# Four alternating GRU chains and four gather buffers in the first stage of a graph network

## The reference

```
h = relu(layernorm(x));  x = x + segment_sum(h[src] * edge_weight, dst)       # round 1
feat = relu(layernorm(x))
4 times:  a = segment_sum((feat @ W[k].T + b[k])[etypes, src], dst)           # round 2
          r = sigmoid(i_r + h_r);  z = sigmoid(i_z + h_z)
          n = tanh(i_n + r * h_n);  feat = (1 - z) * n + z * feat
          # i_* = a @ w_ih.T + b_ih,  h_* = feat @ w_hh.T + b_hh
x = x + feat
```

## Time and profile before

| What | Value |
|---|---|
| Median of three runs | 6666.92 us |
| The profiled execution: its own time | 6632.5 us |
| Its span, first to last instruction | 6630.3 us |
| Busy over the span | PE 64%, DVE 66%, ACT 41%, POOL 64% |
| TensorE's mean granted clock | 0.854 |
| `norm` | 120 to 436 us |
| Node loop without summing, `j` up to 24 | 436 to 1181 us |
| Wait for the first gather of `h[src]` | 1181 to 1416 us |
| Node loop with summing, `j` from 25 | 1416 to about 2600 us |
| First gather of the next stage | 2614.5 us |

### The profile page before, as it was taken

One profiled execution on the slowest core, in us unless ns is written; L12 is line 12 of the kernel. 1 busy time (PEld: TensorE's weight loads), 2 busy tenths in 40 slices (PEclk: granted clock), 3 DMA queues, 4 the chain that ended last, 5 costly groups with the idle time before them and its releaser, 6 DMA issues. The chain is left out here.

```text
span 6630.3 us, 70235 instructions
## 1 busy us (share of the span) xinstructions
PE 4211.2 (64%) x13088; PEld 2105.9 (32%) x13088; DVE 4371.3 (66%) x6372; ACT 2717.9 (41%) x4465; POOL 4255.8 (64%) x3977
## 2 busy tenths in 40 slices
PE   0038888137777776888788788879978882012321
PEld 0014444013434433444344344434434441000110
DVE  3778888137878786777677677767865664455432
ACT  1346666025555554444454444445443331111000
POOL 2666677763333332777677677767767776774777
PEclk9999999568888887999999899999989995555555
DMA  2876554124444443333333333334445552222331
GB/s 82 290 243 209 199 193 162 29 69 142 146 148 140 155 134 121 115 115 118 96 117 114 100 112 116 114 108 140 139 124 133 147 149 79 72 74 77 109 99 57
DMA packets 701757, 843.04 MB, mean 127 GB/s; under 512 B 183377, under 2 KB 339524, under 8 KB 701646
## 3 DMA queue, kind: packets, MB, share of 16 engines
q1 hardware_dynamic: 572286, 716.54, 33.1%
q0 software_dynamic: 129360, 125.36, 8.5%
HBM read 420.11 MB, written 425.30 MB: 128 GB/s over the span
## 5 line engine op out<-in xcount | busy, mean ns | idle before, releaser
L380 POOL DMA_INDIRECT step_g<-f_rows,lab_i x1568 | 1732.3, 1105 | 657.2 <-issue 476.5
L753 POOL DMA_INDIRECT nd_g<-h_and_label,src_i x392 | 419.7, 1071 | 701.8 <-DVE sgn_t L1049 595.1
L1338 DVE COPY_PREDICATED step_msg<-step_mask,step_p_w 128x512 f32<-128x512 uint8 x588 | 427.6, 727 | 518.1 <-ACT step_p_w L1283 487.0
L1240 PE MATMUL step_p_w<-step_gT,wT 128*128 128x512 f32 x1568 | 748.9, 601 | 2.7 <-ACT step_gT L1252 2.7
L731 POOL DMA_INDIRECT nd_xg<-in_x,dst_i x392 | 446.4, 1139 | 389.9 <-DMA x_of_dst<-nd_xg 168.7
L771 PE MATMUL nd_p_r<-nd_fT,wT 128*128 128x512 f32 x588 | 356.3, 690 | 282.4 <-DVE nd_fT L1020 263.9
L1892 POOL DMA_INDIRECT out<-attend_o,last_i x392 | 404.9, 1033 | 178.0 <-issue 119.1
L380 POOL DMA_INDIRECT logits_g<-h_rows,lab_i x392 | 410.5, 1047 | 152.0 <-issue 119.1
L380 POOL DMA_INDIRECT typed_g<-h_rows,lab_i x392 | 403.9, 1030 | 156.7 <-issue 119.2
L744 POOL DMA_INDIRECT h_and_label<-slot,lab_at x392 | 406.8, 1038 | 123.3 <-issue 123.3
L906 ACT ACTIVATE nd_cand<-nd_pre,bias 128x512 f32<-128x512 f32 x392 | 281.9, 719 | 423.9 <-DVE nd_pre L1005 423.9
(11 more groups left out here) (272 smaller groups left out, 9852.6 us busy)
## 6 DMA issues: line engine op xcount, KB each, us to landing
f_rows<-nd_ro SPq DMA_DIRECT2D x294, 256.0 KB
h_rows<-nd_cen SPq DMA_DIRECT2D x98, 512.0 KB
step_mask<-masks SPq DMA_DIRECT2D x392, 128.0 KB
step_fT<-f_turned SPq DMA_DIRECT2D x196, 256.0 KB
f_turned<-step_fn SPq DMA_DIRECT2D x147, 256.0 KB, 2.1
f_rows<-step_rows SPq DMA_DIRECT2D x147, 256.0 KB
h_and_label<-nd_hx SPq DMA_DIRECT2D x49, 528.0 KB, 4.1
f_rows<-nd_h SPq DMA_DIRECT2D x49, 512.0 KB, 3.0
```

The lines of the kernel that those rows point to most:

```text
L380: nc.gpsimd.indirect_dma_start(out=g[:, c % RING, j, :], out_offset=None, in_=table, in_offset=bass.IndirectOffsetOnAxis(ap=idx[:, 8 * c + ...
L753: nc.gpsimd.indirect_dma_start(out=g[:, c % 2, j, :], out_offset=None, in_=m.ht, in_offset=bass.IndirectOffsetOnAxis(ap=m.src_i[:, 8 * c + ...
L1240: pe.matmul(p_w[k % 2][:], lhsT=m.wT[:, WK + k, :], rhs=gT[:, h], start=True, stop=True).then_inc(s_w, 1)
L1338: nc.vector.copy_predicated(msg[:, h], mask[:, h, k], p_w[k % 2][:]).then_inc(s_sel, 1)
```

## The change

The four steps of a pair are spread over two iterations. In iteration `j` the pair `one = j - 1` does its first two steps (stage FIRST) and the pair `two = j - 2` its last two (stage SECOND). The new `slot(k)` gives the stage, the step and the group of slot `k`: even slots are FIRST, odd ones SECOND, and the output of a slot is needed four slots later, or five where it passes to the second stage. So four chains alternate. Work tiles double, and semaphores exist once for each stage. `p_n` has one bank for each stage instead of each group; `p_r`, `p_z`, `p_out` stay single. The loop gets one more iteration at its end. Three orders change too: on DVE `update` is that of the slot before, behind this slot's `argument` and extras; on ACT the candidate stands behind the copy of rows; the addition to `x` and the third norm move from `j - 2` to `j - 3`, the first half of the addition into slot 7 (`add_x`). On POOL `xg` gets four buffers (`RING`), so that the gathers of a chunk wait for the store of the chunk four back instead of two back, and a count `s_moved` tells SP which chunk is in memory. The labels now start once the last store has landed.

```diff
+def slot(k):
+    return k % 2, k // 4, k // 2 % 2
...
-        xg = sb("xg", [P, 2, 8 * D])
+        xg = sb("xg", [P, RING, 8 * D])
...
             def store_x(c):
-                pool.wait_ge(s_xg[c % 2], landed(c, c % 2, 8))
-                nc.gpsimd.dma_start(m.xs[c], xg[:, c % 2]).then_inc(s_xgs[c % 2], 16)
+                pool.wait_ge(s_xg[c % RING], arrived(c, c % RING, 8))
+                nc.gpsimd.dma_start(m.xs[c], xg[:, c % RING]).then_inc(s_xgs[c % RING], 16)
+
+            def stored_x(c):
+                pool.wait_ge(s_xgs[c % RING], arrived(c, c % RING, 1))
+                pool.sem_inc(s_moved, 1)
...
             for c in range(C):
-                if c >= 2:
-                    pool.wait_ge(s_xgs[c % 2], 16 * (c // 2))
+                if c >= RING:
+                    stored_x(c - RING)
...
             store_x(C - 1)
+            for c in range(C - RING, C):
+                stored_x(c)
```

In PE's `body`:

```diff
             def body(j, summing):
-                gru, n2 = j - 1, j - 2
+                one, two = j - 1, j - 2
                 for q in range(8):
-                    if live(gru, NI):
-                        gates(gru, q)
-                    if q < 2 and live(n2, NI):
-                        turn_out(n2, q)
-                    if q >= 2 and live(gru, NI):
-                        turn_out(gru, q)
+                    stage, t, u = slot(q)
+                    if live(two if stage else one, NI):
+                        gates(two if stage else one, stage, t, u)
+                    stage, t, u = slot((q + 6) % 8)
+                    i = (two if stage else one) - (1 if q < 2 else 0)
+                    if live(i, NI):
+                        turn_out(i, stage, t, u)
```

In ACT's `body`:

```diff
                 for q in range(8):
-                    if live(gru, NI):
-                        gate(gru, q)
-                        if q >= 2:
-                            take_rows(gru, q)
+                    here = (two if q % 2 else one, *slot(q))
+                    if live(here[0], NI):
+                        gate(*here)
+                    stage, t, u = slot((q + 6) % 8)
+                    i = (two if stage else one) - (1 if q < 2 else 0)
+                    if live(i, NI) and not (stage == SECOND and t == 1):
+                        take_rows(i, stage, t, u)
+                    if live(here[0], NI):
+                        candidate(*here)
```

In DVE's `body`:

```diff
                 for q in range(8):
-                    if live(gru, NI):
-                        argument(gru, q)
+                    stage, t, u = slot(q)
+                    if live(two if stage else one, NI):
+                        argument(two if stage else one, stage, t, u)
+                    if q == 7 and live(two, NI):
+                        add_x(two, 0)
                     if live(n2, NI):
+                        if q == 1:
+                            add_x(n2, 1)
                         norm2(n2, q)
...
-                    if live(gru, NI):
-                        update(gru, q)
+                    stage, t, u = slot((q + 7) % 8)
+                    i = (two if stage else one) - (1 if q < 1 else 0)
+                    if live(i, NI):
+                        update(i, stage, t, u)
```

More of the change, by code:

```diff
@@ L431, in loop_nodes @@
 def loop_nodes(eng, body):
-    for j in range(3):
+    for j in range(4):
         body(j, False)
-    with eng.Fori(0, TURN - 5) as k:
-        body(k + 3, False)
+    with eng.Fori(0, TURN - 6) as k:
+        body(k + 4, False)
     body(TURN - 2, False)
@@ L486, in nodes_and_sum @@
         p_r, p_z = ps("p_r"), ps("p_z")
-        p_n = [ps(f"p_n{u}") for u in range(2)]
+        p_n = [ps(f"p_n{stage}") for stage in range(2)]
         p_in, p_out = ps("p_in"), ps("p_out")
@@ new lines, in handed_back @@
+                def handed_back(s):
+                    if stage == FIRST:
+                        if is_below(i, 1):
+                            if n > 0:
+                                pe.wait_ge(s[FIRST], n)
+                        elif not (is_below(i, 2) and before == 0):
+                            pe.wait_ge(s[SECOND], 4 * (i - 1) + before)
+                        else:
+                            pe.wait_ge(s[FIRST], n)
+                    elif live(i + 1, NI):
+                        pe.wait_ge(s[FIRST], 4 * (i + 1) + before + 1)
+                    elif n > 0:
+                        pe.wait_ge(s[SECOND], n)
@@ new lines, in gates @@
+                handed_back(s_r)
+                pe.matmul(p_r[:], lhsT=m.wT[:, HR, :], rhs=f, start=True, stop=True).then_inc(s_gr[stage], 1)
+                if not (is_below(i, 1) and before == 0):
+                    pe.wait_ge(s_pre[stage], n)
+                pe.matmul(p_n[stage][:], lhsT=m.wT[:, HN, :], rhs=f, start=True, stop=True).then_inc(s_gn[stage], 1)
+                handed_back(s_z)
+                pe.matmul(p_z[:], lhsT=m.wT[:, HZ, :], rhs=f, start=True, stop=True).then_inc(s_gz[stage], 1)
@@ new lines, in gate, with candidate @@
+                nc.scalar.activation(zg[:, stage, u], p_z[:], ACT.Sigmoid, bias=m.bias[:, B_Z:B_Z + 1]).then_inc(s_z[stage], 1)
+            def candidate(i, stage, t, u):
+                n = 4 * i + 2 * t + u
+                act.wait_ge(s_pre[stage], n + 1)
+                if not (is_below(i, 1) and t == 0):
+                    act.wait_ge(s_f[stage], n - 1)
+                nc.scalar.activation(cand[:, stage, u], pre[:, stage, u], ACT.Tanh, bias=m.bias[:, B_IN:B_IN + 1]).then_inc(s_cand[stage], 1)
@@ L914, in take_f0, with take_rows @@
+            def take_rows(i, stage, t, u):
+                act.wait_ge(s_to[stage], 4 * i + 2 * t + u + 1)
+                if stage == FIRST:
+                    if not (is_below(i, 1) and t == 0):
+                        act.wait_ge(s_ros[stage][u], 32 * i + 16 * t)
+                elif not is_below(i, 1):
+                    act.wait_ge(s_ros[stage][u], 16 * i)
+                nc.scalar.copy(ro[:, stage, u], p_out[:]).then_inc(s_ro[stage], 1)
             def take_f0(j, u):
@@ new lines, in update @@
+            def update(i, stage, t, u):
+                n = 4 * i + 2 * t + u
+                ch = Chain(dve, s_chg[stage], 2 * n)
+                if t == 0:
+                    f = fT[:, FIRST, u, 1, :] if stage == SECOND else f0T[:, u, :]
+                else:
+                    f = fT[:, stage, u, 0, :]
+                c, d = cand[:, stage, u], dif[:, stage, u]
+                dve.wait_ge(s_cand[stage], n + 1)
+                ch.then(nc.vector.tensor_tensor(d, f, c, ALU.subtract))
+                dve.wait_ge(s_z[stage], n + 1)
+                ch.then(nc.vector.tensor_tensor(d, d, zg[:, stage, u], ALU.mult))
+                if not is_below(i, 1):
+                    dve.wait_ge(s_to[stage], n - 3)
+                    if stage == FIRST and t == 1:
+                        dve.wait_ge(s_chg[SECOND], 2 * (4 * (i - 1) + u + 1))
+                nc.vector.tensor_tensor(fT[:, stage, u, t, :], d, c, ALU.add).then_inc(s_f[stage], 1)
@@ L1029, in norm2, with add_x @@
+            def add_x(i, u):
+                if u == 0:
+                    dve.wait_ge(s_xb, 32 + 16 * i if is_last(i, NI) else 16 * i + 16)
+                dve.wait_ge(s_to[SECOND], 4 * i + 3 + u)
+                half = xb[:, 8 * u:8 * u + 8].rearrange("p j d -> p (j d)")
+                nc.vector.tensor_tensor(half, half, p_out[:], ALU.add).then_inc(s_x2, 1)
+            def norm2(i, q):
                 if q == 2:
```

224 lines of the change are left out of this document (103 added, 121 removed).

## The result

The changed kernel takes 6540.84 us (median of 4 runs, 6534.5 to 6547.66), the kernel before took 6663.41 us beside it (6653.81 to 6669.2). The ratio is 0.9818, 95% interval 0.9801 to 0.9835: 123 us or 1.8% faster. The prediction was 6547 us in a range of 6425 to 6625.

A forecast was written before the change was run, and what follows sets the result against it. It took POOL's list alone to bound the kernel up to 1416 us, then the node loop, with no engine full. Its terms, -154 + 0 + 14 + 20 = -120 us, took 6667 us to 6547, range 6425 to 6625.

The forecast's parts named there:

- (1): POOL's x gathers: four buffers end the 168.7 us wait for the store; first weigh 154 us earlier.
- (2): Node loop without summing: stays at 30.5 us an iteration, ends 70 us before the labels, worth nothing.
- (3): Loop with summing: candidate's wait goes, transposes tie PE to DVE; +0.6 us an iteration, +14 us, bounds -178 to +55.
- (4): Tail: the last pair's second stage needs an iteration of its own, +20 us, bounds 10 and 30.
- (5): SP's order, the doubled tiles and a fifth clearing of a tile: move nothing on the path.
- the signs: Marks of a right forecast: last scatter about 1250 us, DVE idle about 80, scans every 24.2, next stage near 2495.
- The waits of the loop vanish: Rival, loop with summing: four chains bring an iteration to 45.5 us or less, -53 to -178 us; chance 0.20.
- The ring brings nothing: Rival, POOL's x gathers: the store's wait moves into the gathers, first weigh stays at 1416 us, 6701 us; chance 0.07.
- The first part binds: Rival, loop without summing: over 33.5 us an iteration uses up the 70 us cover; at 37 us, 6631 us; chance 0.06.
- PE stays slow throughout: Rival, loop with summing: PE slow in all eight slots, 57 us an iteration, +228 us, 6761 us; chance 0.05.

The follow-up runs named there:

- turn_out_later: The changed kernel with each finished state's transposes, copy and additions to x one slot later, three slots behind its gates instead of two: 6417 us, ratio 0.9642 to before.
- chains_only: The changed kernel with two buffers for the gathers of x again, so four chains and nothing else of the change: 6673 us, ratio 1.0032 to before.
- later_no_sqrt: turn_out_later with a Square in place of ScalarE's square root, so the deviation is not the reference's: 6388 us, ratio 0.9599 to before.
- later_root_behind: turn_out_later with the third norm's root behind that slot's two sigmoids and VectorE's scans ahead of the scaling: 6437 us, ratio 0.9685 to before.
- two_chains_later: The kernel before with the four-buffer gather ring and two chains, each output turned one slot later: 6504 us, ratio 0.9774 to before.
- ring_only: The kernel before with four buffers for the gathers of x and nothing else of the change: 6518 us, ratio 0.9801 to before.

## Why the prediction was right, step by step

**(1) The ring: -154 forecast, -141 measured** at the first weigh. The wait for the store went whole, as said. But the idle time in front of the gathers fell by 389.9 - 237.4 = 152.5 us and not by 168.7: where the wait had stood, the gap of issue of some 0.3 us, which it had covered, is seen again: idle time put down to issue rose from 104.8 to 119.1 us, and the first gather started 1.9 us later. A round took (717.5 - 144.9) / 48 = 11.9 us for the 11.7 forecast. The labels, which started at 720.8 and not at about 708, took the 542 us of the forecast to the microsecond (720.8 to 1262.8, the first gather of `h[src]`), with scatters of 1.066 us for 1.038 before, since more of them fall beside the busy loop. The ring without the chains gives -132 at this point, the chains alone -8 and both together -141.

**(2) The loop without summing: 30.5 us forecast, 30.5 measured**, and worth nothing. The tie of `turn_out` is there by its name: 55.7 us of TensorE's waiting in 21 iterations, and it is what held the loop at 30.5, since turn_out_later has 27.7. The loop ended at 1171 us, 10 us earlier than before.

**(3) The loop with summing: 48.3 forecast, 47.8 measured**, +2.5 us over all chunk intervals for the +14 of the sum. `argument`'s starts in one iteration of after were 5.41, 4.02, 6.29, 8.32, 5.34, 4.34, 6.79 and 7.28 us apart, from slot 6 to slot 5, where the forecast had 5.2, 4.5, 6.3, 8.35, 5.3, 4.65, 6.8 and 7.3. The miss is in slots 7 and 3, taken 0.5 and 0.3 us too long. Added up without a slip, the forecast's slots give 48.4 us and not 48.3, +0.7 an iteration and +17 in all for its +14; its lower bound of 45.5 us has no working (with slot 6 at 3.1 us the same slots give 46.3). The mechanism was the one named: the candidate's wait gone, the transposes tied to the last update, 4.56 us of idle, and matmuls at 1.2 GHz behind it; the mean clock 0.86 for 0.84.

**(4) The tail: +20 forecast, +22.4 measured** (68.8 us for 46.4). chains_only shows it by itself: 68.5.

**(5)** Nothing of SP or of the tiles shows up.

The sum for the stage, with -0.3 us between the first weigh and the first scan, is -141.2 - 0.3 + 2.5 + 22.4 = -116.6 us, which is where the next stage starts. The medians say -123. The remaining 6 us are less than the difference between executions.

That the forecast of the time came within 6 us is in part luck. Term (1) promised 13 us too much and term (3) charged 11.5 us too much, and the two nearly cancel. Of the signs, DVE's idle time before the first weigh was 102.8 us and not about 80, because the labels ended 13 us later and the loop 10 us earlier than forecast; the last scatter started at 1260.5 us for "about 1250", the scans came every 23.9 us for 24.2, and the next stage began at 2497.9 for "near 2495".

**The rivals.** *The waits of the loop vanish* did not happen, but its price was real: later_no_sqrt, with the tie loosened and the root left out, is 146 us below after, in a forecast of -53 to -178, although waits for n remain. What spoke against it, the tie and the table loads, is just what the runs showed to hold it back. *The ring brings nothing* fell with the round of 11.9 us. *The first part binds* and *PE stays slow throughout* were not near: an iteration took 30.5 us where the one needs over 33.5, and 47.8 us where the other has 57 (which by its own sum is +223 and not +228 us). The rule of the Trainium skill on a stall that returns in each pass ("TensorE: Matmul & The Clock Gate", HAM oscillation) fits what the traces show: with the 4.56 us stall the loop stays at a granted 0.86, and in turn_out_later, where TensorE hardly waits for fT, the clock rises to 0.90 with summing, and from 0.96 to 1.00 without. It rises no further with summing while other waits remain there, 124.5 us for the weighing among them. And the four chains did cost clock in the loop without summing, which the forecast did not have: 1.00 before, 0.96 in after and in chains_only, with 47 waits for fT of at most 2.0 us in after. The first window is after's, the other two are turn_out_later's:

```profile
509.00:1150.00 641.00, 583.38 (x2020) 302.22 (x2019) 557.28 (x779) 428.68 (x716) 499.05 (x467) 0.96 0.57 187
```
```profile
509.00:1080.00 571.00, 549.04 (x1980) 289.57 (x1979) 542.10 (x765) 414.50 (x703) 440.69 (x415) 1.00 0.62 206
1266.00:2310.00 1044.00, 820.70 (x2906) 455.74 (x2907) 912.91 (x1428) 649.12 (x1013) 411.00 (x383) 0.90 0.50 159
```

How much of the 117 us is the clock and how much the order was not separated: no run held the one and changed the other.

## What to carry to other kernels

Adding chains lengthens the distance between an instruction and its input for some instructions only; list that distance for each one in every queue. Here the gates got two slots more and the transposes between them none, and one instruction that waits for the latest result holds all that are queued behind it: look down the queue of the engine that is waited for, find the instruction whose input is youngest, and move that one first. A hole in which one engine works alone is room for work from behind it: moving the border of the two loops gave 83 us on after. And before an operation that needs its own function table is moved, look at which function comes next behind it: later_root_behind traded two loads for three.

## What the runs showed of the hardware

- With the other engines idle, a gather of 128 rows took POOL 0.99 to 1.01 us and a scatter 0.97 (after, from 1257 to 1274 us); over their whole lists, most of which run beside other work, gathers of `x[dst]` had a mean of 1.12 to 1.18 us and scatters of 1.03 to 1.09, with 0.30 us between two issues. What sets the mean was not found. It does not follow the pace of the node loop beside it: in turn_out_later, with 27.7 us an iteration without summing, gathers and scatters took 1131 and 1045 ns; in two_chains_later, with 31.8 us, 1183 and 1094; in ring_only, with 30.7 us, 1150 and 1072.
- A load of ScalarE's table takes 1.28 us, so the two roots of an iteration bring 5.1 us of loads. Without them after is 76 us faster, 3.2 us an iteration, although ScalarE is busy only 656 of 1154 us. Loads on an engine with 43% of its time free were not hidden; with them gone, VectorE's wait for r was gone too.
- What a root costs in table loads depends on the function behind it. With a sigmoid next, one load served the sigmoid and the candidates after it (turn_out_later: none at L957). With a candidate next, the candidate had a load of its own and the sigmoid behind it another (later_root_behind: 44 each in 960 us).
